# Edge stage of a graph layer: VectorE reads the vector part of the last product in PSUM, and TensorE waits for VectorE's end before the next product

## What is computed

```python
h = silu(edge_scalars @ fc_w1 / sqrt(8)); weight = h @ fc_w2 / 8
f_s, f_v = x_s @ lin1_w0, x_v @ lin1_w1           # per node
gs, gv = f_s[edge_src], f_v[edge_src]
ys, yv = edge_attr[:, :1], edge_attr[:, 1:]
m0a = gs * ys * w1
m0b = sum(gv * yv, -1) * w4 / sqrt(3)
m1a = gs[..., None] * yv[:, None, :] * w2[..., None]
m1b = gv * ys[..., None] * w3[..., None]
mid = segment_sum(concat(m0a, m0b, m1a, m1b), edge_dst) / 4
c_s, c_v = mid_s @ lin2_w0, mid_v @ lin2_w1
angle = 0.1 * (mid_s @ lin3_w) / sqrt(96)
y = layernorm(x + cos(angle) * sc(x) + sin(angle) * concat(c_s, c_v))
```

## Time and profile before

| | before |
|---|---|
| median of 3 runs | 1578.34 us |
| the profiled execution | 1574.12 us |
| its span, first to last instruction | 1572.3 us |
| TensorE matmul busy | 1270.3 us (81%) |
| TensorE weight loads busy | 1119.7 us (71%) |
| VectorE busy | 932.0 us (59%) |
| ScalarE busy | 817.4 us (52%) |
| GpSimd busy | 1294.7 us (82%) |
| mean granted TensorE clock | 0.919 of full |

### The profile page before, as it was taken

One profiled execution on the slowest core, in us unless ns is written; L12 is line 12 of the kernel. 1 busy time (PEld: TensorE's weight loads), 2 busy tenths in 40 slices (PEclk: granted clock), 3 DMA queues, 4 the chain that ended last, 5 costly groups with the idle time before them and its releaser, 6 DMA issues. The chain is left out here.

```text
span 1572.3 us, 28888 instructions
## 1 busy us (share of the span) xinstructions
PE 1270.3 (81%) x8524; PEld 1119.7 (71%) x8524; DVE 932.0 (59%) x4681; ACT 817.4 (52%) x1877; POOL 1294.7 (82%) x1054
## 2 busy tenths in 40 slices
PE   6999999999998777777767666777766718888884
PEld 5888888888887666666666666667656617777774
DVE  4777777777776444444444444434444508999998
ACT  3666666666665333343433333333333404988986
POOL 7777888888888888888878888877788859999997
PEclk9999999999999888888888899878898968999998
DMA  9993444444444444444444454444544458999984
GB/s 368 383 377 82 69 66 67 66 68 68 67 68 65 66 59 58 59 63 63 60 58 59 68 79 74 59 63 61 98 59 59 55 114 367 387 405 398 400 333 178
DMA packets 114761, 220.74 MB, mean 140 GB/s; under 512 B 17264, under 2 KB 77232, under 8 KB 111024
## 3 DMA queue, kind: packets, MB, share of 16 engines
q0 software_dynamic: 75264, 64.68, 30.2%
q1 hardware_dynamic: 27936, 136.82, 22.0%
q10 hardware_dynamic: 11408, 17.39, 4.3%
HBM read 121.43 MB, written 97.40 MB: 139 GB/s over the span
## 5 line engine op out<-in xcount | busy, mean ns | idle before, releaser
L329 POOL DMA_INDIRECT acc<-shared,row_sb x392 | 627.0, 1600 | 135.6 <-issue 104.3
L716 DVE TENSOR_TENSOR shared<-shared 128x192 f32<-128x192 f32 x196 | 70.3, 359 | 549.8 <-ACT shared L581 549.8
L480 PE MATMUL XTZ<-constants_sb,x_shared 128*128 128x128 f32 x588 | 117.7, 313 | 205.2 <-DMA x_shared<-x_odd,src_sb 202.3
L316 POOL DMA_INDIRECT x_shared<-xa,src_sb x196 | 201.3, 1027 | 60.4 <-issue 43.0
L316 POOL DMA_INDIRECT x_shared<-x_odd,src_sb x196 | 199.0, 1016 | 59.7 <-issue 47.2
L480 PEld LDWEIGHTS XTZ<-constants_sb,x_shared 128*128 128x128 f32 x588 | 66.2, 151 | 234.9 <-DMA x_shared<-x_odd,src_sb 221.3
L589 ACT COPY shared<-XTZ 128x384 f32<-128x384 f32 x196 | 93.9, 479 | 260.7 <-PE XTZ L480 260.7
L440 PE MATMUL OC<-constants_sb,shared 128*128 128x193 f32 x784 | 227.6, 376 | 0.0
L423 PE MATMUL OC<-shared 128*128 128x161 f32 x784 | 196.6, 336 | 2.8 <-ACT shared L553 2.1
L553 ACT ACTIVATE shared<-OC,is_last 128x161 f32<-128x161 f32 x392 | 155.3, 396 | 68.4 <-PE OC L427 32.3
L427 PE MATMUL OC<-shared 128*128 128x161 f32 x782 | 188.5, 326 | 0.0
(11 more groups left out here) (92 smaller groups left out, 2686.4 us busy)
## 6 DMA issues: line engine op xcount, KB each, us to landing
acc<-xnt_zeros SPq DMA_DIRECT2D x50, 644.0 KB, 6.7
out<-shared SPq DMA_DIRECT2D x97, 320.0 KB, 10.0
x_shared<-xa SPq DMA_DIRECT2D x13, 2254.0 KB, 11.1
shared<-acc SPq DMA_DIRECT2D x13, 2254.0 KB, 15.9
dstrow_sb<-dst_rows ACTq DMA_DIRECT2D x49, 288.0 KB, 3.6
acc<-shared,row_sb POOLq DMA_INDIRECT x392
x_shared<-x_last SPq DMA_DIRECT2D x13, 448.0 KB, 11.4
x_shared<-xa,src_sb POOLq DMA_INDIRECT x196, 2.8
```

Of the source, the lines that this page charges most:

```text
L316: pool.indirect_dma_start(out=x_sb[:, slot, j * ROWA:(j + 1) * ROWA], out_offset=None, in_=(xa, x_odd)[j], in_offset=bass.IndirectOffsetOn ...
L329: pool.indirect_dma_start(out=acc, out_offset=bass.IndirectOffsetOnAxis(ap=row_sb[:, t:t + 1], axis=0), in_=comb_sb[:, k % RING, j, :], in ...
L480: last = nc.tensor.transpose(XT[:, b * P:(b + 1) * P], x_sb[:, x_slot(a), column:column + P], ident_sb[:, :])
```

## The change

ScalarE copies only the 65 scalar columns of each of the two tiles of OUT to `feat_sb`. VectorE reads the other columns in PSUM: L678 takes its 32 columns there, and L695 takes the 96 vector columns there and writes their sum to `feat_sb`. A row of `feat_sb` shrinks from 193 to 161 columns. Since OUT is now read until L695 is through, TensorE waits before OUT of pair d until `feat_done` has reached d, beside `out_copied`.

```diff
@@ -130,7 +130,7 @@
             return shared[:, at - columns:at]
 
         comb_sb = edge(RING * 2 * ROWA).rearrange("p (s j c) -> p s j c", s=RING, j=2)
-        feat_sb = edge(SLOTS * 2 * OUTW).rearrange("p (s j c) -> p s j c", s=SLOTS, j=2)
+        feat_sb = edge(SLOTS * 2 * ROWA).rearrange("p (s j c) -> p s j c", s=SLOTS, j=2)
         xt_sb = edge(2 * 3 * P).rearrange("p (s c) -> p s c", s=2)
         h_sb = edge(2 * P).rearrange("p (s c) -> p s c", s=2)
         f_sb = edge(2 * 2 * ROW).rearrange("p (s j c) -> p s j c", s=2, j=2)
@@ -435,6 +435,7 @@
                 if 0 <= d < NPAIR:
                     pe.wait_ge(pt_copied, d + 1)
                     wait(pe, out_copied, d)
+                    wait(pe, feat_done, d)
                     for j in range(2):
                         o = j * OUTW
                         nc.tensor.matmul(OUT[:, o:o + OUTW], pt_sb[:, d % 2, (2 + j) * P:(3 + j) * P],
@@ -565,8 +566,8 @@
                 if 0 <= d < NPAIR:
                     act.wait_ge(out_ready, d + 1)
                     wait(act, comb_ready, 2 * (d - SLOTS + 1))
-                    nc.scalar.copy(feat_sb[:, d % SLOTS, :, :], OUT[:, 0:2 * OUTW].rearrange("p (j c) -> p j c", j=2)
-                                   ).then_inc(out_copied, 1)
+                    nc.scalar.copy(feat_sb[:, d % SLOTS, :, NV:ROWA],
+                                   OUT[:, 0:2 * OUTW].rearrange("p (j c) -> p j c", j=2)[:, :, NV:ROWA]).then_inc(out_copied, 1)
                 if 0 <= e < NPAIR:
                     copy_combined(2 * e + 1)
                     if (e + 1) % CHUNK == 0 and (e + 1) // CHUNK + 1 < CHUNKS and (e + 1) // CHUNK + 1 >= ROUNDS:
@@ -673,7 +674,7 @@
             for k in range(NPAIR + 3):
                 d = k - 3
                 if d >= 0:
-                    o = feat_sb[:, d % SLOTS, :, :]
+                    o = OUT[:, 0:2 * OUTW].rearrange("p (j c) -> p j c", j=2)
                     dve.wait_ge(out_copied, d + 1)
                     nc.vector.tensor_tensor(
                         vq_sb[:, :, :, :],
@@ -692,7 +693,7 @@
                             accum_out=later_cnt[:, d % 2, j:j + 1])
                     last.then_inc(same_done, 1)
                     dve.wait_ge(vq_done, d + 1)
-                    nc.vector.tensor_tensor(o[:, :, 0:NV], o[:, :, 0:NV],
+                    nc.vector.tensor_tensor(feat_sb[:, d % SLOTS, :, 0:NV], o[:, :, 0:NV],
                                             vq_sb[:, :, :, :].rearrange("p j c o -> p j (c o)"),
                                             ALU.add).then_inc(feat_done, 1)
                 if k < NPAIR:
```

## The result

The changed kernel takes 2030.77 us, the median of 4 runs (2012.94 to 2054.04), against 1578.47 us, the median of 4 runs of the kernel before. The ratio is 1.2854, with a 95% interval of 1.2819 to 1.2889. The forecast was slower, at 1795 us with a range of 1712 to 1885. The direction came out, and the size was far too small.

A forecast was written before the change was run, and what follows sets the result against it. GpSimd was taken to pace the edge stage. The new ring gave 26.5 + 193 x 7.58 (7.18 plus 0.40 for clock) = 1489 us, then 18 to the last scatter, 286.1 node stage, 1.8 outside the span: 1795 us, range 1712 to 1885.

The forecast's parts named there:

- The old bound: Edge stage before the change: GpSimd's scatters and gathers set the pace at 5.75 us a pair.
- The copy and the PSUM reads: ScalarE's narrower copy saves 0.2 us a pair, booked as nothing; VectorE's multiply and add from PSUM at no added cost.
- The ring: Edge loop: the new wait makes TensorE and VectorE take turns, 7.18 us a turn at full clock.
- TensorE's rest: TensorE stands idle before OUT in each turn, waiting for VectorE's add: nearly 2.4 us.
- The clock in the ring: TensorE's rest brings stretches at 1.2 GHz: 3 turns in 10 at 1.35 us each, 0.40 us a turn.
- The prediction's own sign: Edge stage: the prediction is wrong if TensorE's clock is below 0.8 or stays at 1.00.
- The end: Last pairs: the last scatter ends 18 us after VectorE's L716 of pair 195, at 1507 us.
- The start: Start of the loop: VectorE's L716 of pair 2 at 26.54 us, before the wait holds anyone.
- The node stage: Stage after the last scatter, untouched by the change: 286.1 us as before.
- The upper bound: Low clock in the ring: at most 0.85 us a turn, every second turn at the largest cost.
- The second rival: Edge loop: low clock for part of every turn, 1.8 us in place of 0.40, 2065 us; chance 0.06.
- The chain theory: Experiment filling every fourth turn: a slow turn brings on the next, shares 0, 0.35, 0.54, 0.64, about 1875 us.

The follow-up runs named there:

- the ring cut: Changed kernel with VectorE's multiply and add one turn earlier, or with OUT and its copy behind PT, F and W: 1568.44 and 1563.96 us.
- the add first: Changed kernel with VectorE's add moved ahead of its two comparison instructions: 1654.3 us, ratio 1.0503.

## Why the prediction went wrong, point by point

- **The old bound** (GpSimd with 5.75 us a pair): right. With the ring cut the time is the old one again, and with the ring GpSimd waits.
- **The copy and the PSUM reads** at nothing: right. 269 ns, 350 ns and 352 ns were measured, and the wait alone gives the loss (2026.57 us).
- **The ring** and its 7.18 us at full clock: right. 7.20 us was measured in the full turns of the changed kernel, and 7.21 to 7.22 us with one extra product.
- **TensorE's rest** of nearly 2.4 us: right. It was 2.14 us by the wait row of its matmuls and 2.35 us by that of its weight loads, by which the forecast went.
- **The clock in the ring** at 0.40 us a turn: this step failed. Measured were 142 of 194 turns, slow by 2.29 us on average (9.49 against 7.20), which is 1.67 us a turn. Over 193 turns the difference of 1.27 us is 245 us, and with it the forecast would have been 2040 us. The trace is of the run of 2054.04 us. In the kernel with the wait alone, traced at 2026.79 us, 131 turns were slow. The prediction's own sign, a clock below 0.8 in the edge stage, came out at 0.78.
- **The end** at 18 us from pair 195's first product to the last scatter: 22.1 us (1743.96 to 1766.1), 4 us short. The clock was 0.69 from 1745 to 1750 us and 0.63 from 1750 to 1755 us. **The start**, VectorE's L716 of pair 2 at 26.54: 28.13 us. **The node stage** at 286.1 us: 286.1 us.

Both factors of the failed step were too small. The share, 3 in 10, came from 14 turns of the kernel before whose rest was about as long, and 5 of them were slow. But there a rest of that length stood among others, ahead of XT. In the ring it was 73% with such a rest in every turn, and 46% and 47% with one in every second turn and in three of four. So the old share didn't carry over, and no run shows by what rule it grew.

The price, 1.35 us, came from those five turns, and in all five the clock was low for a short stretch only, which was over before F. This is TensorE's clock (the number behind the brackets) in one of them, in the kernel before:

```profile
647.00:648.00 1.00, 1.00 (x6) 0.50 0.55 74
648.00:649.00 1.00, 1.00 (x6) 0.50 0.00 0
649.00:650.00 1.00, 1.00 (x7) 0.64 0.93 82
650.00:651.00 1.00, 1.00 (x11) 1.00 0.35 68
```

And this is the changed kernel in the turn of 10.13 us shown above, where the clock is at 0.50 from OUT's first weight load (604.04) on:

```profile
604.00:605.00 1.00, 0.93 (x3) 0.50 0.00 0
...
609.00:610.00 1.00, 1.00 (x7) 0.50 0.02 8
610.00:611.00 1.00, 1.00 (x8) 0.86 0.57 46
```

Everything TensorE does from OUT to F then runs at 1.2 GHz and costs 2.9 us more (6.27 against 3.38 us). About half of the slow turns were of this kind. The others had a short low stretch and cost some 1.6 us, nearer to the price assumed. The kernel before had long low stretches too, but only behind the longer rests that the prediction had set aside.

The upper bound of 0.85 us a turn had the same flaw. It took every second turn at the largest cost of those five, and nothing in the rows set that as a limit. The second rival named the right mechanism: low clock as after the longest rests of before, in nearly every turn, 1.8 us each, 2065 us. It had a chance of 0.06 and lay outside the range. That its number comes so near is partly luck, since its share was too large (nearly all against 142 of 194) and its price too small (1.8 against 2.29 us). Its "for" was that the rest now comes in every turn. The Trainium skill (TensorE: Matmul & The Clock Gate, A second HAM failure mode: psum-queue depth-cycling) tells of another kernel in which small rests between groups of matmuls, if they come often enough, make the clock swing between its two levels. The changed kernel agrees, with 142 slow turns of 194 at rests of 2.15 us. With rests of 1.30 us in every turn none was slow.

What stays open is what decides which turn is slow. The rest's length orders the runs with one kind of rest and turns of 7.2 us (2.15 us: 142 of 194, 1.74 us: 5, 1.30 us: none), but 1.48 us in turns of 6.53 us gave 34. The chain theory failed by its shares. Slow turns come in patterns that repeat: 7.21, 7.21, 7.21, 8.8, 10.13, 10.13 in the changed kernel, and every fifth or sixth turn with the add first, where the rests of slow and full turns are alike. This speaks for the moment at which a rest falls, which none of the runs varies by itself.

## What to carry to other kernels

When a wait is added in one engine's hand-written order, ask what is queued behind it and whether the awaited work depends on that. If it does, add up the two shares as one ring, at full clock first. Then price the clock for a rest that comes in every turn and stands on the path, for which single rests of an old trace are no measure. Here that is 1.67 us a turn on a ring of 7.2 us. The cure is to move the awaited instruction a turn earlier or the waiting one behind what others need: the wait itself cost nothing in both.

## What the runs showed of the hardware that I had not expected

- More work made the kernel faster: one useless product a turn (0.86 us of TensorE) took 2031 us to 1728 us.
- In turns of 6.53 us a rest of 1.48 us was enough to bring TensorE to 1.2 GHz in 34 of 194 turns. All 44 turns of the kernel before with rests up to about 1.9 us were at full clock, and 18 of them had rests of about 1.5 to 1.9 us.
- A float32 product of 512 columns took 0.86 us at full clock (2.58 us for three, 605.14 to 607.72).
- The slow turns of the changed kernel came in two kinds, with nothing between. From 300 to 1500 us 46 turns, with a short stretch at 1.2 GHz, took 8.7 to 9.0 us, and 50 turns, with a long one, 10.1 to 10.5 us.
- GpSimd's scatters differed on average with the order and timing of the other engines' work: 1600 ns in the kernel before, 1579 ns with the add a turn earlier and 1577 ns with OUT behind F. Their median was 1572 ns in all three.
